# Edge tables of a graph layer: the duplicate check in groups of 512 edges with keys spread by TensorE, and the last block of destinations in three parts

## What is computed

```python
def _sage_bn_relu(h, src, dst, Wl, bl, Wr, gamma, beta):
    agg = jax.ops.segment_sum(h[src], dst, num_segments=N)
    deg = jax.ops.segment_sum(jnp.ones((src.shape[0],), h.dtype), dst, num_segments=N)
    mean_agg = agg / jnp.maximum(deg, 1.0)[:, None]
    out = mean_agg @ Wl + bl + h @ Wr
    mu = out.mean(axis=0)
    var = out.var(axis=0)
    out = (out - mu) * jax.lax.rsqrt(var + EPS) * gamma + beta
    return jax.nn.relu(out)
...
x = x + _L0_gnn_ref(_layernorm(x, axis=-1), edge_index, ...)   # 256 -> 512 -> 512 -> 256
x = x + _L0_ffn_ref(_layernorm(x, axis=-1)[None], ...)[0]
x = x + _L1_gnn_ref(_layernorm(x, axis=-1), edge_index, ...)
x = x + _L1_ffn_ref(_layernorm(x, axis=-1)[None], ...)[0]
```

## Time and profile before

| | us |
|---|---|
| median of 3 runs | 2953.96 (2953.58 to 2955.12) |
| the profiled execution | 2984.41 |
| its span | 2982.6 |
| first indirect addition | 42.70 |
| last indirect addition issued | 844.86 |
| layer 1 begins (L741) | 879.87 |

### The profile page before, as it was taken

One profiled execution on the slowest core, in us unless ns is written; L12 is line 12 of the kernel. 1 busy time (PEld: TensorE's weight loads), 2 busy tenths in 40 slices (PEclk: granted clock), 3 DMA queues, 4 the chain that ended last, 5 costly groups with the idle time before them and its releaser, 6 DMA issues.

```text
span 2982.6 us, 39397 instructions
## 1 busy us (share of the span) xinstructions
PE 2236.0 (75%) x14137; PEld 1757.0 (59%) x14137; DVE 1282.3 (43%) x2680; ACT 388.3 (13%) x839; POOL 883.3 (30%) x627
## 2 busy tenths in 40 slices
PE   1033100058989989996996888999999996899997
PEld 1022100036667766775775447888888885788886
DVE  7899999955341011111114864212310378111111
ACT  0011000000015000003201221100110002222222
POOL 4888888886830000000001420000000000333332
PEclk9976555579999999998997988999999997999999
DMA  9943333378760999994144000244334443567766
GB/s 345 334 77 47 49 49 50 42 230 271 193 215 0 174 204 189 222 230 98 44 154 138 0 0 1 89 144 142 125 128 154 153 139 118 169 193 207 212 195 176
DMA packets 298821, 425.25 MB, mean 143 GB/s; under 512 B 165858, under 2 KB 235513, under 8 KB 298655
## 3 DMA queue, kind: packets, MB, share of 16 engines
q1 hardware_dynamic: 116575, 295.72, 31.5%
q10 hardware_dynamic: 109760, 108.33, 15.4%
q0 software_dynamic: 72400, 20.04, 7.9%
HBM read 306.57 MB, written 100.17 MB: 136 GB/s over the span
## 4 chain that ended last, share of the span: by engine, by line
PE 52%; POOL 16%; ACTq 12%; DVE 8%; issue 6%; DMA 3%; ACT 2%; DVEq 0%; SPq 0%; POOLq 0%
ACTq L796 11%; POOL at_counts L600 8%; PE ps L2196 8%; PE ps L2197 8%; POOL odd_counts L600 7%; PE ps L2290 7%; PE ps L1897 7%; PE ps L2281 7%; PE ps L1829 4%; PE ps L2028 2%; PE ps L2129 2%; PE ps L2152 2%; PE ps L1915 1%; DMA xrows<-odd_counts 1%; DMA xrows<-at_counts 1%
## 5 line engine op out<-in xcount | busy, mean ns | idle before, releaser
L2196 PE MATMUL ps<-harena,ring 128*128 128x257 f16 (+1 forms) x2500 | 551.5, 272 | 7.7 <-DVE harena L1504 3.6
L2197 PE MATMUL ps<-harena,ring 128*128 128x256 f16 x2500 | 551.3, 271 | 0.0
L1897 PE MATMUL ps<-ring,harena 128*128 128x320 f16 x3800 | 512.5, 297 | 1.4 <-ACT tarena L751 0.8
L1897 PEld LDWEIGHTS ps<-ring,harena 128*128 128x128 f16 x3800 | 371.9, 98 | 138.5 <-issue 3.1
L1118 DVE SCALAR_TENSOR_TENSOR late<-ring,ps 128x1024 f16<-128x1024 f32 x312 | 378.9, 1275 | 12.2 <-DMA ring<-key_rows 10.1
L600 POOL DMA_INDIRECT at_counts<-harena x208 | 330.1, 1587 | 111.4 <-issue 103.7
L600 POOL DMA_INDIRECT odd_counts<-harena x208 | 332.6, 1599 | 63.7 <-issue 62.8
L2196 PEld LDWEIGHTS ps<-harena,ring 128*128 128x128 f16 x2500 | 243.2, 97 | 43.8 <-DVE harena L1542 5.1
L2197 PEld LDWEIGHTS ps<-harena,ring 128*128 128x128 f16 x2500 | 241.7, 97 | 31.1
L654 POOL IOTA harena<- 1x32 int32 x1 | 0.2, 183 | 727.7 <-DVE xrows L1616 727.7
L1921 PE MATMUL ps<-ident,sc 128*1 128x128 f32 x4 | 1.0, 332 | 281.3 <-DVE sc L1064 281.3
(11 more groups left out here) (395 smaller groups left out, 2512.1 us busy)
## 6 DMA issues: line engine op xcount, KB each, us to landing
ring<-at_counts SPq DMA_DIRECT2D x145, 800.0 KB, 4.5
ring<-L_ffn_W SPq DMA_DIRECT2D x64, 1024.0 KB, 5.6
ring<-ad_counts SPq DMA_DIRECT2D x50, 800.0 KB, 4.3
ring<-key_rows SPq DMA_DIRECT2D x52, 512.0 KB, 3.7
at_counts<-tarena ACTq DMA_DIRECT2D x5, 4000.0 KB, 15.2
odd_counts<-tarena ACTq DMA_DIRECT2D x5, 4000.0 KB, 27.2
at_counts<-ring ACTq DMA_DIRECT2D x25, 800.0 KB, 6.9
ad_counts<-xrows ACTq DMA_DIRECT2D x25, 800.0 KB, 8.0
```

Source lines behind the costliest of these rows:

```text
L1897: ins = M(ps[:, 2 * f + h, 0:c], part[:, t, (2 * k + f) * P:(2 * k + f + 1) * P], chunk[q][:, s, h * HB:h * HB + c], start=(t == 0 and par ...
L2196: M(ps[:, i, 0:wide], lhs, hh[:, t, 0:wide], start=(t == 0), stop=False)
L2197: ins = M(ps[:, i, 0:F], lhs, hl[:, t, :], start=False, stop=(t == T - 1))
```

## The change

Groups have 512 edges (GQ = 4), so there are 104 of them, with four indirect DMAs each and the same wait for the previous group of their table. Keys no longer go through HBM: for each group TensorE multiplies a column of the identity, broadcast over 128 columns, by `ekeyT` and so writes the group's 512 keys into every partition of one of PSUM's banks 4 to 7 (`spread_keys`). The comparison reads its keys from there and its weights from SBUF; their copy into PSUM is gone. The statistics of x stand behind sixteen groups (EARLY = 4 turns of four). The two tables have their own zeroing semaphores; POOL looks before groups 0, 8 and 16 whether the blocks that these touch are clear, in each table apart, and before group 24 whether all are. Block 4 has three parts: 320, 117 and 128 columns (the last is loaded 203 wide), each with its own release.

```diff
-NR = NB + 1
+ENDING = P
+PART_AT = (0, HB, N - (NB - 1) * BC - ENDING)
+PART_LOAD = (HB, PART_AT[2] - HB, BC - PART_AT[2])
+PART_USED = (HB, PART_LOAD[1], ENDING)
+PARTS = len(PART_AT)
+NR = NB - 1 + PARTS
-GQ = 8
+GQ = 4
+CHECKS = 3
+EARLY = 4
...
-            sp.wait_ge(keys_dve, 1)
-            sp.dma_start(key_rows.rearrange("(p c) -> p c", c=RW), ekeyT).then_inc(key_stored, 16)
-            sp.wait_ge(key_stored, 16)
-            for s in range(LOOK):
-                sp.dma_start(krow[:, s, :], key_rows[s * GE:(s + 1) * GE].partition_broadcast(P)).then_inc(piece_in[s], 16)
+            sp.wait_ge(odd_zeroed, 32)
             sp.dma_start(xrows[:, 0:T - 1, :], x[0:(T - 1) * P, :].rearrange("(t p) d -> p t d", p=P)).then_inc(x_in, 16)
...
+            for h in range(PARTS):
                 released(0, NB - 1 + h)
+                if h > 0:
+                    sp.wait_ge(tables_summed, (NB - 1 + h) * NB)
                 for q in range(NB):
-                    load_half_even(q, h)
+                    load_part_even(q, h)
                 released(1, NB - 1 + h)
                 for q in range(NB):
-                    load_half_odd(q, h)
+                    load_part_odd(q, h)
...
             for g in range(0, NG, 2):
-                if g == FIRST_GROUPS:
-                    pool.wait_ge(zeroed, 32 * (NB + 1))
+                check = g % FIRST_GROUPS == 0 and g <= CHECKS * FIRST_GROUPS
+                if check:
+                    blocks_cleared(g // FIRST_GROUPS, even_zeroed)
                 add_group(g, at_flat, even_added)
+                if check:
+                    blocks_cleared(g // FIRST_GROUPS, odd_zeroed)
                 add_group(g + 1, odd_flat, odd_added)
...
+            for b in range(1, NB):
+                if b == NB - 1:
+                    ln_sqrt(1)
+                act.wait_ge(even_zeroed, 16 * (b + 1))
+                clear(at, even_zeroed, b)
+                act.wait_ge(odd_zeroed, 16 * (b + 1))
+                clear(odd, odd_zeroed, b)
...
-            step(V.tensor_copy(weight_ps, eweight))
...
-                    dve.wait_ge(piece_in[s], i * 16 + (16 * ahead + 16))
+                    dve.wait_ge(keys_spread, i * LOOK + (ahead * LOOK + s + 1))
...
-                        ins = V.scalar_tensor_tensor(out=ejunk[q], in0=krow[:, s, :], scalar=ekey[:, bass.ds(g + q, 1)], in1=weight_ps[:, GE - P - q * P:2 * GE - P - q * P],
+                        ins = V.scalar_tensor_tensor(out=ejunk[q], in0=ps[:, LOOK + s, :], scalar=ekey[:, bass.ds(g + q, 1)], in1=eweight[:, GE - P - q * P:2 * GE - P - q * P],
...
+            def spread_keys(turn):
+
+                for g in range(turn * LOOK, (turn + 1) * LOOK):
+                    if turn > 0:
+                        pe.wait_ge(compared, g + 1 - LOOK)
+                    M(ps[:, LOOK + g % LOOK, :], ident[0:ER, g:g + 1].to_broadcast([ER, P]), ekeyT, start=True, stop=True).then_inc(keys_spread, 1)
```

More of the change, by code:

```diff
@@ L189, in build @@
         eweight = ring[:, 832:832 + 2 * GE - P]
[L190 to L193, removed]
+        ejunk = [late[:, q * GE // 2:(q + 1) * GE // 2].bitcast(fp16) for q in range(GQ)]
         ecount = ring[:, 7872:7872 + 4 * GQ].rearrange("p (a c) -> p a c", a=4)
@@ L710, in _ @@
             act.dma_start(wl2[:, 0:2, :], w["L0_gnn_Wl0"].rearrange("(d p) f -> p d f", p=P)).then_inc(w0_in, 16)
-            for b in range(1, NB):
-                act.wait_ge(zeroed, 32 * (b + 1))
-                clear(at, b)
-                clear(odd, b)
             def ln_sqrt(k):
@@ L772, in _ @@
                 b, q = n // NB, n % NB
-                wait(tables_summed, n + 1 if b < NB - 1 else n + NB + 1)
+                wait(tables_summed, n + 1 if b < NB - 1 else n + (PARTS - 1) * NB + 1)
                 if n >= 2:
@@ L1000, in _ @@
             dve.wait_ge(fold_pe, 1)
-            step(V.tensor_reduce(first_block, ps[0:1, 1, 0:2 * FIRST_GROUPS], AX.X, ALU.max))
-            step(V.tensor_scalar(release[:, 3, 0:1], first_block, 32.0, 64.0, ALU.mult, ALU.add))
+            for k in range(CHECKS):
+                o.mark(V.tensor_reduce(first_block[:, k:k + 1], ps[0:1, 1, 0:FIRST_GROUPS * (k + 1)], AX.X, ALU.max))
+            o.settle()
+            step(V.tensor_scalar(release[:, 3, 0:CHECKS], first_block, 16.0, 32.0, ALU.mult, ALU.add))
             V.tensor_copy(ekey.rearrange("p (r a) -> p a r", a=RQ), ps[:, 0, 0:EC].rearrange("p (a r) -> p a r", a=RQ)).then_inc(keys_dve, 1)
@@ L1092, in block_releases @@
                 o.settle()
-                step(V.scalar_tensor_tensor(out=eflt[:, 3, :], in0=eflt[:, 1, :], scalar=float((NB - 1) * BC + HB), in1=eflt[:, 3, :], op0=ALU.is_ge, op1=ALU.add))
+                for part_at in PART_AT[1:]:
+                    step(V.scalar_tensor_tensor(out=eflt[:, 3, :], in0=eflt[:, 1, :], scalar=float((NB - 1) * BC + part_at), in1=eflt[:, 3, :], op0=ALU.is_ge, op1=ALU.add))
                 for b in range(NR):
@@ L1131, in _ @@
             edges_of(0, 0, range(2, LOOK))
-            edges_of(0, 1)
+            for turn in range(1, EARLY):
+                edges_of(0, turn)
             dve.wait_ge(x_in, 32)
@@ L1308, in _ @@
                 if l == 0:
-                    for h in range(2):
+                    for h in range(PARTS):
                         for q in range(NB):
-                            sum_half(q, h)
-                        aggregated_half(h)
+                            sum_part(q, h)
+                        aggregated_part(h)
                 else:
@@ L1843, in enter_block @@
                     half_products(l, b, h, weights, HB if h == 0 else last)
+            for turn in range(1, EARLY):
+                spread_keys(turn)
             pe.wait_ge(keys_dve, 3)
@@ L1853, in _ @@
             pe.wait_ge(fold_dve, 6)
-            with pe.Fori(0, NB) as b:
+            for b in range(NB):
+                spread_keys(b + EARLY)
                 pe.wait_ge(rows, b * BT + BT)
@@ L1863, in _ @@
                 products(b)
+            for turn in range(NB + EARLY, NG // LOOK):
+                spread_keys(turn)
             def nothing_between(q):
```

186 lines of the change are left out of this document (92 added, 94 removed).

## The result

The changed kernel takes **2929.86 us** (median of 4 runs, 2927.35 to 2930.67), the one before 2954.54 on the same chip: ratio **0.9909**, 95% interval 0.9888 to 0.9929. The forecast was 2945, 8.6 us less; measured are 24.7 less. On a second chip the changed kernel measured 2929.92.

The account below looks back on a forecast made before the run. Two nearly meeting limits: POOL's 416 additions (772.9 us) and DVE's comparisons, which delay table loads. With -0.2 us at POOL's end and -8.4 behind it, 2953.96 - 8.6 = 2945.4, say 2945; own range 2938 to 2952, outer 2928 to 2963.

Parts of the forecast that it names:

- The start: Front of layer 0: without the keys' way through HBM, POOL's first addition comes at 23.7 us, 19.0 us earlier.
- (a): POOL's checks that table blocks are cleared: about 1 us each, five more of them, 5 us lost.
- (b): TensorE's fold at the front, no longer hidden by a ten-us group: the second group's indices come late, 2 us lost.
- (c): During zeroing, landings over 8.5 us stall POOL because groups hold fewer additions: 0 to 17 us, taken as 4.
- (d): Table loads slow POOL's additions, in bursts after indices end near 430 us: 34 us lost, against 26 before.
- POOL's end: End of POOL's additions in layer 0: 846.2 us by the sum of terms, as good as unchanged from 846.4.
- the scattered 4.6: POOL's small losses kept from the profile before: 2.5 us spread over the rest and 2.1 in the first stretch.
- The end: First odd load of the last part to layer 1: 23.5 us, 1.5 for the clock, instead of 31.9; 8.4 gained.
- Rival 1: Slower: POOL's landing waits in bursts and zeroing take back the gain, +18 us on the forecast, 2963; chance 0.20.
- Rival 2: Nothing: narrower rows or a late part 1 keep the end at 32.5 us, 2954 in all; chance 0.12.
- Rival 3: More: shorter groups do not stall and bursts cost as before, so POOL ends earlier, 2933; chance 0.18.

Follow-up runs that it names:

- experiment 2: The changed kernel with 39 more checks (register load and met wait) ahead of POOL's groups: 2930.27 us, ratio 0.9894.
- experiment 6: The changed kernel with the key store and 104 broadcast key loads put back, read by nobody: 2936.3 us, ratio 0.9932.
- experiment 7: The changed kernel with POOL also waiting for the other table's previous group ahead of each group's third addition, slack 4.8 instead of 8.5 us: 2969.66 us, ratio 1.0054.
- experiments 4: The changed kernel with the last block in two parts again (320 and 245 columns): 2939.63 us, ratio 0.9947.
- experiment 5: The kernel before with groups of 512 edges instead of 1024, keys still spread by broadcast loads from memory: 2952.33 us, ratio 0.9987.
- experiment 9: The changed kernel with SyncE issuing the last block's stores, ScalarE's root no longer behind them: 2929.2 us; then also with a last part of 65 columns: 2923.5 us.
- experiment 8: The changed kernel with POOL's load of Wr1 put behind the last sum: 2933.2 us; then also with a last part of 65 columns: 2931.18 us.

## Why the prediction was right in sign and short in size

- **The start, gain 19.0.** Right: 18.4. DVE and TensorE do as foretold.
- **(a) Checks, 5 us.** Wrong, 0. The 1 us was read from the first addition, where POOL truly waits; behind an addition that takes 1.55 us POOL's sequencer reads the register meanwhile (experiment 2).
- **(b) Fold, 2.** 1.2.
- **(c) Landing wait in the zeroing, 4.** 0 in the changed kernel. The slack of 8.5 us was right, the landing was taken from a row of before, in which the key loads ran; the long landings, 11.0 at most in that row, made the term. I counted their removal only at the start, not in the queues. With them the wait costs 5.3 us (7.5 against 2.2 by the 64th addition, experiment 6).
- **(d) Table loads, 34.** 30.3, all that is lost behind the 240th addition, of it 17.1 in waits and 13.2 in additions longer than 1.55 us. I had put both down to landings, by a median of 17.7 us. That row is of 622 to 675 us alone; between 700 and 800 us the median was 5.0. And while the first stretch before (622 to 692) has 14.3 us of waits, the last one (692 to 847), whose 10.1 us I kept as well, has none: its additions are longer. The burst's waits stayed at 14.1 us with half the slack. The burst came at 470, not 430, and held three blocks; the later blocks found TensorE idle as foretold. That landings in a saturated stretch don't depend on how many are outstanding was wrong: in experiment 7, with fewer outstanding, they were quicker.
- **POOL's end.** The failed step is this sum: "the start's 19 us are spent". It ends at 829.6, not 846.2. By the table 2.9 us are lost up to the 240th addition, where 15.6 were foretold (2.5 + 2.1 + 5 + 2 + 4), and 30.3 behind it instead of 34: 16.4 too much, (a) and (c) 9 of them, the fold 0.8 and the loads 3.7. The remaining 2.9 are the scattered 4.6: up to the 240th addition the kernel before itself loses only 2.6 us, and the changed one 1.7 without the fold. Some 2 of the 4.6 belong to the time of the loads, where (d) already had its share.
- **The end, 23.5.** 24.0. Within it errors cancel, which is luck: five sums are done 10.2 us behind the first odd load (12.0 foretold), TensorE ends 6.3 us behind them (3.5 foretold, 1.5 of it for the clock), and 7.4 follow (8.0). PE's granted clock, after 23.5 us without a matmul, was 0.50 from 838 to 843.5, the lower of its two levels (1.2 and 2.4 GHz), and 0.94 from 843.5 to 849; 20 matmuls took 2.34 and then 1.34 us. Three chunks begin 7.0 us apart in sum where the later ones are 1.42 apart, so the clock costs 2.7 us.
- **Rival 1** did not come; experiment 7 shows its mechanism, at half the slack. **Rival 2** did not come: narrower rows never made the last loads later. With Wr1 beside them, the last of five sums ends 10.0 to 12.0 us behind the first load at 640 B a row (the kernel before, experiments 4 and 5), 9.6 to 10.3 at 406 B, and 8.8 at 280 B (experiment 9); with Wr1 out of the way 8.1 at 406 B and 6.7 at 280 B (experiment 8). From 640 to 406 B the gain is near 1 us and hardly clear of the scatter; the 1.8 us against the kernel before overstate it. The Trainium skill ("DMA: Bandwidth & Descriptors", Specifications) wants 512 B for line rate; the prediction took from it that a narrower load would be no shorter, and here it was somewhat shorter. At what rate these rows move, no run here shows. **Rival 3** is what came, by its own reason for a part: "shorter groups do not stall at all". It had 0.18 and should have had more, since the change itself removed the traffic.

By experiments 5, 4 and the result the gain splits into 2.1 us for the size, 12.7 for TensorE's spreading (with what came with it: the earlier start, the clears' order, the checks) and 9.7 for the parts. The last is a difference between chips; on one chip, and in the tail, the parts are worth 7 to 8.

## What to carry to other kernels

A duration read from the trace holds for the traffic that ran beside it; when an edit removes a transfer, ask which landings it made long, before pricing a wait by them. A queue engine that a burst throws off its period gets it back if the loads are issued in pace with it, where the consumer has idle time later. When a second path ends 3 us ahead of the first, shortening the first by more shows little: read both ends from the trace, and look which transfers the edit moves beside the second.

## What the runs showed of the hardware that was not expected

- POOL reads a register and takes a met wait at no cost that shows behind an indirect DMA instruction: with 39 checks more the gaps stay at 0.30 us and the median moves by 0.4.
- A comparison of 512 columns takes 746 ns with the keys in PSUM and the weights in SBUF, and 744 ns the other way round (experiment 5).
- The landing of an addition follows the load: 2.7 us in the quiet stretch, 7.6 beside the clears, 8.4 with key loads too, 11.5 in the burst's first 60 us (medians).
- Beside table loads an addition can also take longer itself, 2 to 3.2 us instead of 1.55, without any wait: 10.8 of the burst's 24.9 us, and all that was lost in the last stretch before.
